# Mamba scan inside a transformer block: the output projection from f16 halves with a factor per chunk, one step later

## The chip, the core, the metric

The kernel runs on one core of a Trainium2 chip. Times are device microseconds of one execution. Before the change: median 766.98 us of 3 runs, 766.56 to 767.13.

## The reference, cut to what matters

```
x = x + 0.5 * ffn(layernorm(x))          # stage 1, dequantized 512x512 weight plus LoRA
h = layernorm(x)
h = h + mamba2(rmsnorm(h)) ; x = x + h + mlp(rmsnorm(h))     # stages 2 and 3
x = x + 0.5 * ffn(layernorm(x))          # stage 4
# in mamba2, 16 chunks of 128 tokens, 4 heads of 128:
Y = (att @ Xdt) + C @ state * exp(cs) + D * x ;  y = Y * silu(z) ;  return y @ w_out.T
```

x is 2048 tokens by 512, float32. `y @ w_out.T` is a product of 128 tokens by 512 with a 512x512 weight for each chunk: this is the output projection that the change is about.

## The kernel before, in words

Activations stay in SBUF with 128 partitions. Most products are computed from f16 halves: an f32 operand is scaled by a power of two and split into a high f16 part (ACT writes it) and a low part (DVE writes value minus high), and a product is hi*hi + hi*lo + lo*hi. The helper `product` (L1957) issues these three matmuls per block of 128 of the contraction; all of them are recorded at L1960. For four blocks that makes twelve matmuls of 512 columns.

The scan runs over 16 chunks, `step(c)`, c = 0 to 15, four chunks to a group i of 512 tokens, j = c mod 4. Every engine (`tensor`, `vector`, `scalar`, `gpsimd`, and `sync` for DMA) has its own list of instructions, written out by hand in a function `step(c)`; what an engine does is fixed in order, and semaphores (`e_...`) tie the lists. Work for later chunks is put between: stage 1 for chunk c+8 (`f`, `x1_stats`, `hi0`, `lo0`, `hi1`, `lo1`; steps 0 to 7 only), the input projections of group i+1 (`proj`, `SLOTS`: three, two, three and two of them in the steps j = 0 to 3; j = 0 has the dt columns, `steps`, as well), the convolution and gates of these (`conv`, `tanh` on ACT, `taps`, `silu`, `silu_z`, `softplus` on DVE), and in the last group the first gate/up products of stage 3 (`gate_up`). In steps 10 to 14 POOL also forms sums for Strassen's scheme in stage 3 (`sums`, `t_op`), DVE their low halves (`t_los`), and in steps 11 and 12 the halves of the first gate, up and down weights are cut (`cut_a`, `cut_b`).

One chunk goes this way. PE: `s1(c+1)`, `f`, `s2_diag` (L2056, needs the masked scores S from POOL), `s2_state` (L2065), `s2_inner` (L2073), `s1_bc(c+1)` (L2048), one projection or gate/up product, `w(c)` (L2083), the other projections. DVE: `gate_y` (L1425) multiplies Y by the gate, in place and in f32; `advance` (L1432) makes the next state; `weights` (L1406), `scan1` (L1415) make the next scores; POOL masks them and adds the diagonal (`scan_d`, L553, L555). `w(c)` is four f32 matmuls from y and the f32 `w_out`. `residual2(c)` (L1441) adds the normalized input n1 to it and `square` (L803), `rms2` (L559, L521), `hi2` (L794), `lo2(c)` (L1376) and a DMA transpose (`t2`, L457) make the next stage's input, hi2 and lo2 in step c+1.

PSUM banks 0 to 2 rotate among f, w and the projections in the order of `PLAN` (L289 to 320); a product waits until what used its bank three products before has been read.

Of the kernel before, what the change touches and what calls it, by code (L numbers as in the profile page):

```python
# [27 lines left out]
def build(nc, x_in, w_in_t, conv_w, conv_b, a_log, d_skip, dt_bias, w_out_t, ln1_w, ln2_w,  # L28
# [23 lines left out]
    with ctx:  # L52
# [8 lines left out]
        w_out = sb("w_out", [P, H, DM])  # L61
# [17 lines left out]
        homes = [gated_home(t) for t in (stage[:, 0:2048], stage[:, 2048:4096], w_out[:, :, :].rearrange("p h n -> p (h n)"))]  # L79
# [56 lines left out]
        q_raw = early.bitcast(I32)[:, 0:KB, DM:2 * DM]  # L136
        wf = early[:, KB:2 * KB, DM:2 * DM]
# [71 lines left out]
        wv = sb("wv", [P, 2, H])  # L209

# [11 lines left out]
        DT_AT, COL_AT, ROW_AT = 2 * P, 2 * P + 32, 3 * P  # L222

# [21 lines left out]
        def tokens_of(t, c):  # L245
# [15 lines left out]
        e_x_bn, e_x_var, e_x_rstd, e_x_scale, e_n0_hi, e_n0_lo, e_n0_tr = (  # L261
            sem(n) for n in "e_x_bn e_x_var e_x_rstd e_x_scale e_n0_hi e_n0_lo e_n0_tr".split())
        e_n0T, e_ffn, e_x1, e_x1_bn, e_x1_var, e_rms1, e_hn_scale = (
            sem(n) for n in "e_n0T e_ffn e_x1 e_x1_bn e_x1_var e_rms1 e_hn_scale".split())
# [10 lines left out]
        e_x2, e_ssq, e_ms, e_rms2, e_h2_hi, e_h2_lo = (  # L275
            sem(n) for n in "e_x2 e_ssq e_ms e_rms2 e_h2_hi e_h2_lo".split())
# [6 lines left out]
        e_scx, e_wscale, e_dsx, e_descale, e_c_var, e_c_rstd, e_c_scale = (  # L283
            sem(n) for n in "e_scx e_wscale e_dsx e_descale e_c_var e_c_rstd e_c_scale".split())
        e_cn_hi, e_cn_lo, e_cffn, e_c_bias, e_out, e_c_bn = (
            sem(n) for n in "e_cn_hi e_cn_lo e_cffn e_c_bias e_out e_c_bn".split())
# [19 lines left out]
        for c in range(NCH):  # L306
            i, j = divmod(c, CH)
            if c + 2 * CH < NCH:
                put(("f", c + 2 * CH), (e_x1, c + 2 * CH + 1))
            if c == 2 * CH + 2:  # L310
                put(("mx", 0), (e_scx, 1))
            if i + 1 < NS:
                put_proj(i + 1, SLOTS[j][0])
# [3 lines left out]
            put(("w", c), (e_x2, c + 1), None if i + 1 < NS else B_P[2])  # L317
            if i + 1 < NS:
                for q in SLOTS[j][1:]:
                    put_proj(i + 1, q)  # L320
# [77 lines left out]
        def _(sp_):  # L398
# [23 lines left out]
            sp_.dma_start(w_out[:, :, :], w_out_t.rearrange("(h p) n -> p h n", p=P)).then_inc(s_wout, 16)  # L422

# [3 lines left out]
            sp_.dma_start(ln2[:, :], ln2_w).then_inc(s_small, 16)  # L427
            gate_v = gate_t.rearrange("(k p) f -> p k f", p=P)
# [50 lines left out]
            for c in range(NCH):  # L479
# [6 lines left out]
                if c > 0:  # L486
                    t2(c - 1)
                if a < NCH:
                    t1(a)
                    next_x(a)  # L490
            t2(NCH - 1)
# [20 lines left out]
        def _(po):  # L512
# [13 lines left out]
            def ln0(c, j):  # L526
                po.wait_ge(e_x_var, c + 1)
                rsqrt(r0[:, c:c + 1], mv0[:, c, 2:3]).then_inc(e_x_rstd, 1)
                po.wait_ge(e_x_rstd, c + 1)
# [8 lines left out]
            def ln1_chain(c, j):  # L538
                po.wait_ge(e_x1_var, c + 1)
                rsqrt(r1[:, c, :], mv1[:, c, 2:4]).then_inc(e_rms1, 1)  # L540
                po.wait_ge(e_rms1, c + 1)
# [14 lines left out]

            def rms2(c, j):
                po.wait_ge(e_ssq, c + 1)
                po.tensor_scalar(ms[:, c:c + 1], ssq[:, c:c + 1], DOWN / DM, EPS * DOWN, ALU.mult, ALU.add).then_inc(e_ms, 1)  # L559
                po.wait_ge(e_ms, c + 1)  # L560
# [13 lines left out]
            chain(po.memset(ones3[:, :], 1.0))  # L574
            chain(po.memset(ident[:, :], 0.0))
# [48 lines left out]
            def step(c):  # L624
                a = c + 2 * CH
                if a < NCH:
                    ln1_chain(a, a % CH)
                if c + 1 < NCH:
                    scan_c(c + 1, (c + 1) % CH)
                    scan_d(c + 1, (c + 1) % CH)  # L630
                if a + 1 < NCH:
# [3 lines left out]
                early_sums = c in (3 * CH, 3 * CH + 1)  # L635
                if early_sums:
                    sums(c)
                rms2(c, c % CH)
                if not early_sums:
                    sums(c)  # L640

            def sums(c):
                for n in T_EARLY.get(c, ()):
# [4 lines left out]
                       3 * CH + 1: range(12, 16), 3 * CH + 2: range(16, 20)}  # L648
# [67 lines left out]
            for n in range(4, N_TOP):  # L716
# [13 lines left out]
            def c_norm(c, k):  # L730
                po.wait_ge(e_c_var, c + 1)
                rsqrt(rC[:, c:c + 1], mvC[:, c, 2:3]).then_inc(e_c_rstd, 1)
                po.wait_ge(e_c_rstd, c + 1)
# [23 lines left out]
        def _(ac):  # L757
# [43 lines left out]
            def square(c, j):  # L801
                ac.wait_ge(e_x2, c + 1)
                ac.activation(junk[:, :], x2[:, j % 2, :], ACT.Square, accum_out=ssq[:, c:c + 1]).then_inc(e_ssq, 1)  # L803

# [123 lines left out]
            def step(c):  # L928
# [11 lines left out]
                if a + 1 < NCH:  # L940
                    hi0(a + 1, (a + 1) % CH)
                if c > 0 and i_late < NS:
                    for q in late[1:]:
                        slot_b(i_late, q)
                if 0 < c <= 3 * CH:
                    hi2(c - 1, (c - 1) % CH)
                if c + 1 < NCH:
                    scan_decay(c + 1, (c + 1) % CH)
                if c > 3 * CH:
                    hi2(c - 1, (c - 1) % CH)  # L950
                if j == 2 and i + 1 < NS:
                    slot_a(i + 1, SLOTS[j][0])
                if a < NCH:
                    hi1(a, a % CH)
                if c + 1 < NCH:
# [3 lines left out]
                renorm(c)  # L959
                if c == 3 * CH + 2:  # L960
                    t_his(1, 0, 1, 2, 3)
                if i + 1 < NS:
                    if j != 2:
                        slot_a(i + 1, SLOTS[j][0])
                    slot_b(i + 1, SLOTS[j][0])
                    if j == 0:
                        sp_exp(i + 1)
                else:
                    gate_a(0, j)
                    gate_b(0, j)  # L970
                square(c, j)
# [9 lines left out]
            def prologue():  # L981
# [1432 lines left out]
```

## Time and profile before

| | |
|---|---|
| profiled execution | 768.65 us, its span 766.9 us |
| PE busy | 755.4 us, 98% of the span |
| DVE, ACT, POOL busy | 626.5, 446.4, 337.2 us |
| granted TensorE clock | full in all 40 slices |
| w_out's DMA, 1024 KB | 12.5 us from issue to landing |
| fourth block of the ffn weight made | at 18.5 us (DVE L1311, start 17.82, 0.69 long) |
| a DMA transpose of h2n_p | 2.7 us to landing in the median |

PE's matmuls are pipelined: the record of one reaches into the next, so what one costs in the stream is the difference between the starts. An f32 matmul is two records. The scan's steps take up the span from about 88 to 338 us, stage 3 follows, stage 4 is the end.

### The profile page before, as it was taken

The numbers are of one execution on the slowest core, as the hardware profiler recorded it, in microseconds if no ns is written. First come the engines' busy times: TensorE is split into PE (matmuls) and PEld (weight loads), VectorE is DVE, ScalarE is ACT, GpSimd is POOL, SyncE is SP. The second block draws the span as 40 slices with busy tenths as digits, with TensorE's granted clock in tenths as the row PEclk, the third lists the DMA queues.
The fourth block names the chain that finished last, engine by engine and source line by source line (L and its number), as shares of the span: only waits on it lengthen the run. The fifth ranks groups of instructions, "written<-read, shape, count | busy, mean of one in ns | idle before, by whom it ended". The sixth has DMA issues, their size and how long they took to land.

```text
span 766.9 us, 10654 instructions
## 1 busy us (share of the span) xinstructions
PE 755.4 (98%) x3469; PEld 353.2 (46%) x3470; DVE 626.5 (82%) x1230; ACT 446.4 (58%) x881; POOL 337.2 (44%) x392
## 2 busy tenths in 40 slices
PE   8999999999999999999999999999999999999998
PEld 3444554454555444444443444444444444444443
DVE  6888878878878979878799978878878878767994
ACT  3877767766686766643545556456456456444441
POOL 5631534663442379775413333233233233224574
PEclk9999999999999999999999999999999999999999
DMA  8843543552321211420521743743743743443565
GB/s 311 171 75 71 139 94 83 110 111 60 78 56 28 42 38 42 114 55 1 124 47 23 172 77 64 163 77 62 164 77 65 162 77 66 79 77 69 119 169 138
DMA packets 95414, 71.86 MB, mean 94 GB/s; under 512 B 65232, under 2 KB 72400, under 8 KB 95360
## 3 DMA queue, kind: packets, MB, share of 16 engines
q0 software_dynamic: 17280, 31.46, 23.0%
q1 hardware_dynamic: 77600, 39.66, 19.5%
q8 instruction: 28, 0.46, 0.2%
q14 instruction: 26, 0.21, 0.1%
q10 hardware_dynamic: 480, 0.07, 0.1%
HBM read 20.32 MB, written 4.19 MB: 32 GB/s over the span
## 4 chain that ended last, share of the span: by engine, by line
PE 77%; DVE 13%; ACT 4%; issue 3%; POOL 2%; DMA 1%; ACTq 0%; POOLq 0%; DVEq 0%
PE PS L1960 64%; PE PS L2083 4%; PE PS L2183 3%; DVE raw L1450 2%; PE PS L2091 1%; DVE stage L1450 1%; PE PS L2056 1%; DVE state L1432 1%; PE PS L2065 1%; DVE st L1289 1%; PE PS L2073 1%; PE PS L2048 1%; DVE xs L1382 1%; DVE S L1415 1%; DMA h<-lora_b_t 1%
## 5 line engine op out<-in xcount | busy, mean ns | idle before, releaser
L712 POOL DMA_DIRECT2D xs<-x x59 | 50.9, 864 | 151.2 <-ACT x L1159 137.1
L1960 PE MATMUL PS<-h,w_in 128*128 128x512 f16 x480 | 108.7, 379 | 0.2 <-issue 0.2
L1960 PE MATMUL PS<-h,x_t 128*128 128x512 f16 x408 | 94.0, 379 | 0.0
L1960 PEld LDWEIGHTS PS<-h,w_in 128*128 128x128 f16 x480 | 46.9, 98 | 65.3 <-issue 15.5
L1960 PE MATMUL PS<-n_T,stage 128*128 128x512 f16 x288 | 71.5, 379 | 0.0
L1159 ACT ACTIVATE x<-PS,d_d 128x512 f32<-128x512 f32 x59 | 40.2, 682 | 39.1 <-PE PS L1960 39.1
L1960 PEld LDWEIGHTS PS<-h,x_t 128*128 128x128 f16 x408 | 39.5, 98 | 48.5 <-issue 2.3
L521 POOL TENSOR_TENSOR r<-mv,mhalf 128x1 f32<-128x1 f32 (+1 forms) x32 | 29.4, 917 | 72.2 <-DVE mv L1293 55.0
L712 POOL DMA_DIRECT2D xs<-n x29 | 25.2, 868 | 71.1 <-ACT n L1159 60.8
L1960 PE MATMUL PS<-pre,stage 128*128 128x512 f16 x192 | 49.3, 379 | 0.0
L1129 ACT ACTIVATE xds<-tm,dgh 128x512 f32<-128x512 f32 x24 | 17.3, 722 | 53.0 <-DVE tm L1889 53.0
L1960 PEld LDWEIGHTS PS<-n_T,stage 128*128 128x128 f16 x288 | 28.1, 98 | 34.0 <-ACT x L1159 0.3
L1960 PE MATMUL PS<-w_ffn,raw_gu 128*128 128x512 f16 x192 | 43.2, 379 | 0.0
L1450 DVE SCALAR_TENSOR_TENSOR raw<-pre,cw,raw 128x512 f32<-128x512 f32 x36 | 28.0, 777 | 10.4 <-ACT raw L885 10.1
L1960 PE MATMUL PS<-raw,x_t 128*128 128x512 f16 x144 | 34.7, 379 | 0.4 <-DVE Ld L1842 0.4
L1960 PE MATMUL PS<-w_in,x_t 128*128 128x512 f16 x144 | 34.8, 379 | 0.0
L1159 ACT ACTIVATE n<-PS,d_d 128x512 f32<-128x512 f32 x29 | 19.8, 683 | 23.8 <-PE PS L1960 22.5
L1960 PE MATMUL PS<-h,n 128*128 128x512 f16 x144 | 33.2, 379 | 0.3 <-DVE n L1530 0.3
L2083 PE MATMUL PS<-w_out,stage 128*128 128x512 f32 x64 | 29.3, 600 | 0.3 <-DVE stage L1425 0.2
L1960 PEld LDWEIGHTS PS<-pre,stage 128*128 128x128 f16 x192 | 18.7, 98 | 22.7 <-ACT x L1159 0.3
L1960 PEld LDWEIGHTS PS<-w_ffn,raw_gu 128*128 128x128 f16 x192 | 18.7, 98 | 22.7 <-DMA raw_gu<-h2n_p 0.3
L2083 PE MATMUL PS<-w_out,raw 128*128 128x512 f32 x64 | 29.0, 595 | 0.1
(314 smaller groups left out, 1819.3 us busy)
## 6 DMA issues: line engine op xcount, KB each, us to landing
xs<-x POOLq DMA_DIRECT2D x75, 256.0 KB, 3.3
xs<-n POOLq DMA_DIRECT2D x29, 256.0 KB, 3.3
x_t<-x_in SPq DMA_DIRECT2D x16, 256.0 KB, 3.0
x_t<-hb POOLq DMA_DIRECT2D x16, 256.0 KB, 3.8
out<-x_t SPq DMA_DIRECT2D x16, 256.0 KB, 2.3
raw_gu<-gate_t SPq DMA_DIRECT2D x7, 512.0 KB, 4.4
raw_gu<-up_t SPq DMA_DIRECT2D x7, 512.0 KB, 6.6
raw_d<-down_t SPq DMA_DIRECT2D x7, 512.0 KB, 7.3
```

The source lines that it names most:

```text
L521: return po.tensor_tensor(dst, src, mhalf[:, 0:src.shape[-1]], ALU.pow)
L712: po.dma_start(chunk_of(xs, c), d_tmps[d % 3], accum_op=ALU.add).then_inc(s_acc[d % 3], 16)
L1129: ac.activation(th_s[ab], u4 if ab else c11, ACT.Tanh, scale=dgh[:, p % 2:p % 2 + 1]).then_inc(e_tanh_g, 1)
L1159: ac.activation(d_tmps[d % 3], bank(d_bank(d)), ACT.Copy, scale=d_d[:, p % 3:p % 3 + 1]).then_inc(e_ev, 1)
L1289: link(ve.bn_stats(stat, src), e_link, base + 1)
L1382: link(ve.scalar_tensor_tensor(chunk_of(xs, c), bank(b), 0.5 / ACT_SCALE if c < NF else d_f[:, :], x_t[:, j, :], ALU.mult, ALU.add), e_x1, ...
L1415: last = ve.scalar_tensor_tensor(S[:, s, h, :], heads(B_G)[:, h, :], dt[:, (c // CH) % 2, j * H + h:j * H + h + 1], Ld[:, h, :], ALU.mult, ...
L1432: last = ve.scalar_tensor_tensor(state[:, h, :], state[:, h, :], ecs[:, s, h, P - 1:P], heads(B_SS)[:, h, :], ALU.mult, ALU.add)
L1450: ins = ve.scalar_tensor_tensor(xbc[i % 2][:, b, :], pre[:, w, k:k + ST], cw[:, b, k:k + 1], xbc[i % 2][:, b, :], ALU.mult, ALU.add)
L1960: ins = pe.matmul(out_, lhs(a, b, k), rhs(a, b, k), start=first and n == 0, stop=last and n == len(todo) - 1)
L2083: last = pe.matmul(bank(b), y[:, h, (c % CH) * P:(c % CH + 1) * P], w_out[:, h, :], start=h == 0, stop=h == H - 1)
L2183: last = pe.matmul(bank(B_P[c % 2]), nT32[c % 2][:, k, :], wf[:, k, :], start=k == 0, stop=k == KB - 1)
```

## The change

- `w_out` is kept as two f16 halves. Its DMA goes to a raw place and is issued later, behind the making of the ffn weight. In the prologue ACT sums the absolute values of each row (`wo_sum`), DVE turns the sum into a power of two per partition (`wo_scale`), ACT writes the high half (`wo_hi`), DVE the low half (`wo_lo`, four times). `gate_y` multiplies by the inverse of that factor.
- y of a chunk is scaled by a factor of the chunk: ACT squares and sums y (`y_sum`), PE spreads the sum over all partitions with an f32 matmul of one column (`y_over`, into the bank of the state product), DVE reads it (`y_max`), POOL takes it to the powers -0.5 and 0.5 (`y_scale`), ACT writes y's high half (`y_hi`), DVE the low one (`y_lo`).
- `w(c)` is a `product` of these halves, twelve f16 matmuls, and stands in step c+1 behind `s1_bc`, ahead of the projections. `renorm(c)`, `residual2(c)` and `square(c)` go to step c+1 as well, residual2 ahead of `advance`; `rms2`, `hi2`, `lo2` and the transpose go to step c+2. `residual2` multiplies by the chunk's factor on the way.
- `s2_inner` waits for `y_max` of the chunk before, where it waited for `advance`.
- POOL's sums of step 14 move behind the scan; `sums` is always the last of a step. `w(15)` stands behind the fifth gate/up product.
- Some links of an engine with itself use the engine's own counter instead of a semaphore each.

```diff
-        w_out = sb("w_out", [P, H, DM])
+        w_out = sb("w_out", [P, 2, H, DM], F16)
...
+            def y_scale(c):
+                po.wait_ge(e_ym, c + 2)
+                po.tensor_tensor(y_s[:, c, :], y_m[:, c, :], halves[:, :], ALU.pow).then_inc(e_yscale, 1)
...
+                if c > 1:
+                    rms2(c - 2, c % CH)
                 if a < NCH:
                     ln1_chain(a, a % CH)
                 if c + 1 < NCH:
                     scan_c(c + 1, (c + 1) % CH)
                     scan_d(c + 1, (c + 1) % CH)
+                y_scale(c)
...
-                early_sums = c in (3 * CH, 3 * CH + 1)
-                if early_sums:
-                    sums(c)
-                rms2(c, c % CH)
-                if not early_sums:
-                    sums(c)
+                sums(c)
...
+            def y_sum(c):
+                ac.wait_ge(e_y, c + 1)
+                if c > 1:
+                    ac.wait_ge(e_ssq, c - 1)
+                ac.activation(junk[:, :].rearrange("p (h t) -> p h t", h=H), y_of(c), ACT.Square, accum_out=ssy[:, c:c + 1]).then_inc(e_ysum, 1)
+
+            def y_hi(c):
+                ac.wait_ge(e_yscale, c + 1)
+                if c > 0:
+                    ac.wait_ge(e_wo, c)
+                ac.activation(y_hl[:, 0, :, :], y_of(c), ACT.Copy, scale=y_s[:, c, 0:1]).then_inc(e_yhi, 1)
...
+            def y_max(c):
+                ve.wait_ge(e_yall, c + 1)
+                ve.tensor_scalar(y_m[:, c, :], PS[:, B_SS, 0:1].broadcast_to([P, 2]), Y_TINY, None, ALU.max).then_inc(e_ym, 1)
+
+            def y_lo(c):
+                cols = slice((c % CH) * P, (c % CH + 1) * P)
+                ve.wait_ge(e_yhi, c + 2)
+                ve.scalar_tensor_tensor(y_hl[:, 1, :, :], szs[(c // CH) % 2][:, :, cols], y_s[:, c, 0:1], y_hl[:, 0, :, :],
+                                        ALU.mult, ALU.subtract).then_inc(e_ylo, 1)
...
-                if 0 < c <= 3 * CH:
-                    lo2(c - 1)
+                if c > 0:
+                    residual2(c - 1, (c - 1) % CH)
+                if 1 < c <= 3 * CH:
+                    lo2(c - 2)
                 advance(c, j)
...
-                if j == 2 and i + 1 < NS:
-                    residual2(c, j)
+                y_max(c)
                 if i + 1 < NS:
                     slot_a(i + 1, SLOTS[j][0], {1: 9}.get(j))
...
                 else:
                     gate_up(0, j)
-                if j != 2 or i + 1 == NS:
-                    residual2(c, j)
+                y_lo(c)
...
                 pe.wait_ge(e_xds, c + 1)
                 if c > 0:
-                    pe.wait_ge(e_state, c)
+                    pe.wait_ge(e_ym, c + 1)
...
-                pe.wait_ge(e_y, c + 1)
+                pe.wait_ge(e_ylo, H + c + 1)
                 pe.wait_ge(*freed)
-                for h in range(H):
-                    last = pe.matmul(bank(b), y[:, h, (c % CH) * P:(c % CH + 1) * P], w_out[:, h, :], start=h == 0, stop=h == H - 1)
-                last.then_inc(e_wo, 1)
+                product(bank(b), lambda a, b, h: y_hl[:, a, h, :], lambda a, b, h: w_out[:, b, h, :], H).then_inc(e_wo, 1)
+
+            def y_over(c):
+                pe.wait_ge(e_ysum, c + 2)
+                pe.wait_ge(e_state, c + 1)
+                pe.matmul(PS[:, B_SS, 0:1], ssy[:, c:c + 1].broadcast_to([P, P]), over[:, :], start=True, stop=True).then_inc(e_yall, 1)
...
                 if c + 1 < NCH:
                     s1_bc(c + 1)
+                if c > 0:
+                    w(c - 1)
...
-                    for q in SLOTS[j][1:]:
+                    for n, q in enumerate(SLOTS[j][1:]):
                         proj(i + 1, q)
+                        if n == 0:
+                            y_over(c)
```

## Rows read from the trace of the kernel before

**Rows 1.** The page: busy time of each engine.
```profile
PE 755.4 (98%) x3469; PEld 353.2 (46%) x3470; DVE 626.5 (82%) x1230; ACT 446.4 (58%) x881; POOL 337.2 (44%) x392
```

**Rows 2.** Timeline of PE, steps 5 and 6: start, duration, line, operation.
```profile
175.01 2.75 PE L1960 MATMUL PS<-w_ffn,n_T 128*128 128x512 f16 x12
177.60 1.02 PE L2056 MATMUL PS<-S,tm 128*128 128x512 f32 x2
...
181.07 2.75 PE L1960 MATMUL PS<-h,w_in 128*128 128x512 f16 x12
183.92 3.70 PE L2083 MATMUL PS<-w_out,raw 128*128 128x512 f32 x8
187.46 2.75 PE L1960 MATMUL PS<-h,w_in 128*128 128x512 f16 x12
...
199.15 0.29 PE L2012 MATMUL PS<-dA,tri 128*128 128x16 f32 x2
199.29 0.43 PE L2013 MATMUL PS<-tri,dA 128*80 128x128 f32 x2
```

**Rows 3.** Timeline of PE: two waits, in steps 10 and 12.
```profile
253.71 0.27 PE L2124 MATMUL PS<-ident,mx 128*3 128x128 f32 x1 [0.52 <-ACT raw L885]
...
284.21 1.13 PE L2056 MATMUL PS<-S,tm 128*128 128x512 f32 x2 [1.02 <-POOL S L555]
```

**Rows 4.** Stretches: steps 1-7, 8-11, 12-15; length, busy time of each engine.
```profile
106.40:223.30 116.90, 116.52 (x542) 57.88 (x541) 98.74 (x239) 84.82 (x192) 56.14 (x69) 1.00 0.38 78
223.30:282.60 59.30, 58.43 (x289) 29.38 (x288) 49.06 (x114) 40.51 (x101) 24.55 (x28) 1.00 0.20 41
282.60:338.00 55.40, 54.35 (x225) 26.61 (x224) 46.62 (x77) 32.72 (x72) 46.06 (x44) 1.00 0.31 70
```

**Rows 5.** Timeline of DVE: taps, lo2, advance, weights, and cut_b's first part.
```profile
234.19 2.33 DVE L1450 SCALAR_TENSOR_TENSOR raw<-pre,cw,raw 128x512 f32<-128x512 f32 x3 [1.13 <-ACT raw L885]
236.43 0.23 DVE L1573 SCALAR_TENSOR_TENSOR sp<-PS,d_i,dtb 128x16 f32<-128x16 f32 x1
...
248.45 0.75 DVE L1376 SCALAR_TENSOR_TENSOR h2n_p<-x,r,h2n_p 128x512 f16<-128x512 f32 x1
249.11 1.12 DVE L1432 SCALAR_TENSOR_TENSOR state<-state,ecs,PS 128x128 f32<-128x128 f32 x4
250.15 0.16 DVE L1406 TENSOR_TENSOR wv<-Ld,dt 128x4 f32<-128x4 f32 x1
...
299.50 2.64 DVE L1509 SCALAR_TENSOR_TENSOR x_t<-raw_gu,sw,x_t 128x512 f16<-128x512 f32 x2
```

**Rows 6.** Timeline of POOL: a two-column pow, scan_d of step 9, sums of step 11.
```profile
200.92 1.09 POOL L521 TENSOR_TENSOR r<-mv,mhalf 128x2 f32<-128x2 f32 x1 [5.63 <-DVE mv L1293]
...
251.44 0.63 POOL L553 TENSOR_SCALAR_AFFINE_SELECT S<-S 128x512 f32<-128x512 f32 x1 [5.68 <-DVE S L1415]
252.16 1.27 POOL L555 TENSOR_TENSOR S<-S,d_diag 128x512 f32<-128x512 f32 x1
...
285.83 1.53 POOL L678 TENSOR_TENSOR h2n<-n_p,h2n 128x512 f32<-128x512 f32 x1
...
291.57 1.27 POOL L549 TENSOR_TENSOR raw<-raw,ecs 128x512 f32<-128x512 f32 x1
```

**Rows 7.** Timeline of ACT: a squared sum, a high half.
```profile
283.54 0.63 ACT L803 ACTIVATE junk<-x 128x512 bf16<-128x512 f32 x1 [2.01 <-DVE x L1441]
...
287.75 0.72 ACT L794 ACTIVATE h2n_p<-x,r 128x512 f16<-128x512 f32 x1
```

**Rows 8.** Line L1376 alone, ns min/median/max; then its group from 88 to 338.
```profile
L1376 DVE SCALAR_TENSOR_TENSOR h2n_p<-x,r,h2n_p x16: 735/752/2519, 115.6 to 336.5; 128x512 f16<-128x512 f32 x16
...
L1376 DVE SCALAR_TENSOR_TENSOR h2n_p<-x,r,h2n_p 128x512 f16<-128x512 f32 x16 | 17.3, 1081 | 5.0 <-ACT h2n_p L794 4.9
```

**Rows 9.** Timeline of ACT in the prologue: two waits for PE.
```profile
45.38 0.20 ACT L864 ACTIVATE pre<-hist 128x3 f32<-128x3 f32 x1 [3.11 <-PE PS L1960]
...
70.34 0.20 ACT L883 ACTIVATE pre<-hist 128x3 f32<-128x3 f32 x1 [3.57 <-PE PS L1960]
```

More of the change, by code:

```diff
@@ L209, in build @@
         wv = sb("wv", [P, 2, H])
+        y_hl = sb("y_hl", [P, 2, H, P], F16)
+        over = sb("over", [P, 1])
+        halves = sb("halves", [P, 2])
+        ssy = sb("ssy", [P, NCH])
+        y_m = sb("y_m", [P, NCH, 2])
+        y_s = sb("y_s", [P, NCH, 2])
+        wo_s = sb("wo_s", [P, 4])
         PS = ctx.enter_context(nc.psum_tensor("PS", [P, 8, 512], F32))
@@ L574, in _ @@
             chain(po.memset(ones3[:, :], 1.0))
+            chain(po.memset(over[:, :], 2.0 ** (-2 * Y_TOP)))
+            chain(po.memset(halves[:, 0:1], -0.5))
+            chain(po.memset(halves[:, 1:2], 0.5))
             chain(po.memset(ident[:, :], 0.0))
@@ L715, in _ @@
                 step(c)
-            for n in range(4, N_TOP):
+            rms2(NCH - 2, CH - 2)
+            for n in range(2):
+                t_op(2, n)
+            rms2(NCH - 1, CH - 1)
+            for n in range(2, N_TOP):
                 t_op(2, n)
@@ L949, in step @@
                 if c > 3 * CH:
-                    hi2(c - 1, (c - 1) % CH)
+                    hi2(c - 2, c % CH)
+                y_late = j != 2 and c < 2 * CH - 1
+                if not y_late:
+                    y_sum(c)
                 if j == 2 and i + 1 < NS:
@@ L954, in step @@
                     hi1(a, a % CH)
+                if y_late:
+                    y_sum(c)
+                if c > 0:
+                    square(c - 1, (c - 1) % CH)
                 if c + 1 < NCH:
@@ L969, in step @@
                     gate_a(0, j)
+                    y_hi(c)
                     gate_b(0, j)
-                square(c, j)
                 if i + 1 < NS:
@@ L1176, in _ @@
                 step(c)
+            hi2(NCH - 2, CH - 2)
+            gate_a(0, EARLY_GU)
+            renorm(NCH - 1)
+            gate_b(0, EARLY_GU)
+            square(NCH - 1, CH - 1)
             hi2(NCH - 1, CH - 1)
-            gate_a(0, EARLY_GU)
-            gate_b(0, EARLY_GU)
             for part in range(3):
@@ L1917, in c_out @@
                 ve.scalar_tensor_tensor(o_t[k], bank(k), d_f[:, :], chunk_of(xs, c), ALU.mult, ALU.add).then_inc(e_out, 1)
+            lo2(NCH - 2)
             gate_up(0, EARLY_GU)
+            residual2(NCH - 1, CH - 1)
             scale_read(1)
```

132 lines of the change are left out of this document (83 added, 49 removed).

## The prediction

> **What bounds the kernel now.** I read the page first: PE is busy 755.4 of 766.9 us [rows 1], so whatever TensorE issues less of is worth its time, as long as nobody makes it wait. Then TensorE's timeline through one step of the scan; the reader is to take the difference between one start and the next, not the durations, since matmuls overlap [rows 2]. Twelve f16 matmuls run from 175.01 to 177.60, 2.59 us. The scan's products of step 5 and the next chunk's score product run from there to 181.07, 3.47 us. The projection behind them takes 183.92 - 181.07 = 2.85, of which 2.59 is its twelve matmuls and 0.26 is waiting for the gated y. The output projection, four f32 matmuls in eight records, takes 187.46 - 183.92 = 3.54 us.
>
> Third, TensorE's own waits in the scan. They are short; two of the longest stand in steps 10 and 12, 0.52 and 1.02 us, the second ahead of L2056, where a step's masked scores come from DVE through POOL [rows 3]. So behind a full TensorE there is a second chain that is nearly as long. Fourth, the stretches [rows 4]: DVE is busy 98.74 of 116.90 us in steps 1 to 7, 49.06 of 59.30 in steps 8 to 11 and 46.62 of 55.40 in steps 12 to 15, 84, 83 and 84%. POOL is at 48% in the first and at 83% in the last. The bound is PE, with DVE two to three microseconds per step below it.
>
> **The change, part by part.**
> *The projection.* Twelve f16 matmuls for four f32: 3.54 - 2.59 = 0.95 us where these rows stand. The other bound is 0.88: the 3.47 us above are three f32 products of 512 columns and one of four times 128, so nearly the same work without the change of kind. I take 0.90 for sixteen, 14.4 us off PE.
> *The factor's matmul* (y_over, sixteen). One f32 matmul with one moving column. The nearest row is L2012 with 16 columns: 199.29 - 199.15 = 0.14 us [rows 2]. Bounds 0.1 and 0.29, the latter the whole duration of L2012's record. At 0.14, 2.2 us. PE's work thus falls by 12.2 us (between 9.4 and 13.6).
> *DVE.* Per chunk it gains y_lo, the same form as lo2 (249.11 - 248.45 = 0.66 in the stream), and y_max, a 128x2 read of PSUM: 0.2, by the 128x4 row's 0.16; bounds 0.1 and 0.4. residual2 becomes 0.07 longer. About 0.95 us a step. In steps 1 to 15 DVE then needs 194.4 + 14.3 = 208.7 us of what would be 231.6 - 11.4 = 220.2 on PE: 95% [rows 4, 5].
> *ACT* gains y_sum (0.63, and a read of the accumulator) and y_hi (0.72): 21 us over the scan, beside idle time of 32.1, 18.8 and 22.7 [rows 4, 7]. *POOL* gains a two-column pow, 1.09, in the stream 1.15 [rows 6].
> *Prologue.* The weight's absolute sum and its high half are 2048 columns on ACT each, some 2.5 us by four of the 512-column row; the low halves are four 0.66 on DVE. I count them at nothing: ACT stands idle 3.11 us ahead of 45.38 and 3.57 ahead of 70.34 [rows 9], exactly where the two are put, and the weight's DMA, issued when the fourth ffn block is made (18.5) and landing 12.5 later (table), is there before 42. Without that cover they cost up to 3 us; I keep 1 in the range.
> *Semaphores that become links within an engine* (statistics, rsqrt): the same waits, nothing, within 1 us either way.
>
> **What is queued where.** The factor ties the engines together inside a step. y_over(c) on PE stands behind the step's second projection, 7.8 us after the score product of c+1 (w and two projections), and waits for advance(c) and y_sum(c). DVE's y_max(c) waits for it, in front of the taps of the step's first projection; the next state product waits for y_max(c). Old DVE ran from gate_y(c) into advance(c) without needing more of PE; now residual2(c-1) stands before advance, and waits for w(c-1), 2.59 us behind the score product.
>
> I walked the four queues, each instruction starting at the later of "engine free" and "wait met", durations from rows 2, 5, 6 and 7.
> Steps 8 and 9: let the score product of step 8 end at 0. w ends at 2.6, a projection at 5.2, the dt columns (1.2) at 6.4, a projection at 9.0, y_over at 9.1. y_max 9.4; three taps, 2.24 to the next start, 11.6; three softplus links 0.6; y_lo 12.8; silu 13.4. Then DVE waits for ACT's conv of the next projection (y_hi and tanh ahead of it) until 13.9; two groups of taps with softplus, 2.4 each, and gate_y 0.66: 19.4. Two silus with 0.7 of waiting for tanh between them 21.2; residual2 21.9, lo2 22.5, advance (1.04) 23.6, scan1 (four like advance's) 24.7; POOL's mask and add, 2.0 us from 251.44 on [rows 6]: 26.7. PE reaches that product at 24.1 and stands 2.6 us, against 0.5 before. What was saved on PE in these two steps is gone.
> Step 12: y_max(11) stands behind cut_a, so y_scale(11) begins only then, and behind it on POOL the four sums, 285.83 to 291.57, 5.7 us [rows 6]. rms2(10) follows them, then hi2(10), and in step 12 the decay, lo2(10) and advance wait for that: 1.8 us at y_over(12). In step 13 advance stands behind cut_b, 2.64 us in its first part alone [rows 5]: another 1.8; then 0.9 for y_lo.
> All steps: 2.6 us given back in steps 0 to 7 (1.4 of it at y_over(6)), 2.0 more in 8 to 11, 8.8 in 12 to 15 and at the exit to the second stage, 13.4 in all. Sum: -12.2 + 13.4 = +1.2 us. The profiled execution took 768.65 (766.9 and 1.75 around it), which becomes 769.85; it lies 1.67 above the median of 766.98, so the median becomes 768.2.
>
> *A rule against the change.* lo2's form takes 0.735 us at the least, 0.752 in the median, 2.519 at the most, and sixteen of them were busy 17.3 us, mean 1.08 [rows 8]; the long ones lie beside POOL's tensor operations. By this mean y_lo, which has the same form, costs 16 x (1.08 - 0.75) = 5.3 us more than I counted. The Trainium skill ("SBUF — State Buffer", section "Who interferes with whom") says that a Vector instruction with two SBUF inputs and a GpSimd instruction that reads SBUF exclude one another for a whole instruction. The trace agrees in direction. What the walk leaves out is which new low halves meet a sum; that is rival B.
>
> **The rivals.**
> (A) *PE stays fed.* For it: PE's busy time lacks only 0.4, 0.9 and 1.1 us of the three stretches [rows 4], and the additions to ACT and POOL find idle time. Against: DVE needed at 95%. If some 5 of the 12.2 us are given back: -7 us, 760.
> (B) *The new low halves meet POOL's sums* (the other side). Place: steps 10 to 15, where POOL is 83% busy. Price: the 5.3 us, two thirds of them not hidden since each also delays advance or scan1: 3.5 on the forecast's 1.2, 771.7. It decides once DVE has no idle time left in a step, above 1 us of lengthening per step.
> (C) *The exit.* w(15) and the last rms2, hi2, lo2 come behind one more gate/up product; the last transposed chunk is needed two products (10.4 us) after w(15). Chain: residual2 0.7, square 0.7, rms2 0.9, hi2 0.7, lo2 0.7, the transpose 2.7 (table): 6.4. It holds unless POOL's sums, 1.3 each, stand in front. Late: +3 us, 771.
> (D) *It doesn't do what it says*: w stays at 3.5 us, twelve weight loads costing what the f32 passes did. The f16 products in rows 2 speak against it. +13.4 + 1.2, of which waits hide half: 775.
>
> **How the numbers follow.** What this measurement tells from no change is 0.2%, 1.5 us: 765.5 to 768.5. Forecast (saving given back, -2.5 to +4 about +1.2) 0.46: faster 0.07, same 0.24, slower 0.15. A 0.29: all faster. B 0.15, C 0.07, D 0.03: slower but for 0.02, which is same. Faster 0.36, same 0.26, slower 0.38. Range: down to 759, A with part of its tail; up to 774, B with the upper bounds of y_max and the prologue. The likeliest case alone is 764.5 to 771.
>
> **What would show it.** Right: w at L1960 and 2.59 us per chunk; PE's waits in the scan at about 13 us, most of them in steps 12 to 15, ahead of L2056, y_over and w; DVE over 90% busy in the scan; DVE waiting for PE at y_max in the steps with dt columns; steps 8 and 9 no shorter than before. Wrong: PE waiting under 8 us in the scan, so that DVE's idle time was slack and not queue, with a time of 762 or less; or waits that stand behind the last chunk.

## The result, and the profile after

| | before | after |
|---|---|---|
| median | 766.83 us (766.56 to 767.13, 4 runs) | 785.43 us (783.55 to 786.39, 4 runs) |
| profiled execution, its span | 768.65, 766.9 us | 786.39, 784.4 us |
| PE busy | 755.4 us, 98% | 753.0 us, 96% |

The ratio is 1.0236, 95% interval 1.0224 to 1.0248: slower by 18.6 us, where 768.2 was forecast and 774 was the upper end of the range.

The page after, busy time of each engine (it answers [rows 1]), and the granted clock in 40 slices:

```profile
PE 753.0 (96%) x3565; PEld 353.7 (45%) x3566; DVE 643.1 (82%) x1271; ACT 471.1 (60%) x932; POOL 358.9 (46%) x411
...
PEclk9999999999998999999999999999999999999999
```

PE's busy time fell by 2.4 us only, and the 13th slice, 235 to 255 us, has a lower clock. The three stretches of [rows 4], after, cut at the same instructions (length, busy us of PE, PEld, DVE, ACT, POOL; then granted clock, DMA share, GB/s):

```profile
102.05:218.11 116.06, 111.78 (x584) 57.19 (x582) 103.19 (x258) 95.42 (x219) 66.29 (x77) 1.00 0.39 78
218.11:283.74 65.63, 58.95 (x315) 30.32 (x314) 53.41 (x121) 44.20 (x109) 29.04 (x32) 0.95 0.18 37
283.74:351.14 67.40, 58.31 (x252) 27.75 (x251) 48.99 (x88) 39.60 (x88) 45.27 (x45) 0.92 0.32 63
```

They took 116.90, 59.30 and 55.40 us before. PE stands idle 4.3, 6.7 and 9.1 us in them, 20.1 in all, where it was 2.3. Fifteen w and fifteen y_over lie in them, so its busy time should have fallen by 11.4 us (15 times 0.76, w's 0.90 less y_over's 0.14) and fell by 0.3. What was saved was lost again, most of it at the lower clock.

Where the 17.5 us of span are, by marks that both timelines have. The dt columns of step 0 begin at 95.56 us (96.48 before): 0.9 earlier. Those of step 8 begin at 227.91 (230.13): 2.2 earlier. The first product of stage 3 begins at 359.33 (343.86): 15.5 later. The end is 17.5 later. So steps 8 to 15 with the exit lost 17.7 us and stage 3 another 2.0.

TensorE's timeline after, the new pieces and the waits (start, duration, line, operation; in brackets the idle time before, and its releaser):

```profile
99.36 0.28 PE L2169 MATMUL PS<-over,ssy 128*128 128x1 f32 x2
99.50 2.75 PE L2045 MATMUL PS<-h,w_in 128*128 128x512 f16 x12
...
108.67 2.75 PE L2045 MATMUL PS<-w_out,y_hl 128*128 128x512 f16 x12
111.26 1.03 PE L2045 MATMUL PS<-h,w_in 128*128 128x512 f16 x4
...
247.52 0.35 PE L2169 MATMUL PS<-over,ssy 128*128 128x1 f32 x2 [1.16 <-DVE state L1510]
...
249.67 0.38 PE L2211 MATMUL PS<-ident,mx 128*3 128x128 f32 x1 [1.32 <-DVE mx L1544]
250.60 2.08 PE L2141 MATMUL PS<-S,tm 128*128 128x512 f32 x2 [0.56 <-POOL S L565]
252.47 1.92 PE L2150 MATMUL PS<-stage,state 128*128 128x128 f32 x8
...
274.86 1.13 PE L2133 MATMUL PS<-raw 128*128 128x512 f32 x2 [3.08 <-DVE raw L1536]
...
286.38 1.67 PE L2141 MATMUL PS<-S,tm 128*128 128x512 f32 x2 [2.04 <-POOL S L565]
...
313.61 0.35 PE L2169 MATMUL PS<-over,ssy 128*128 128x1 f32 x2 [3.02 <-DVE state L1510]
313.82 4.44 PE L2045 MATMUL PS<-h,x_t 128*128 128x512 f16 x12
...
344.27 7.04 PE L2045 MATMUL PS<-h,x_t 128*128 128x512 f16 x24 [2.12 <-DVE pre L1879]
```

The reader is to see two things. The terms of the sum are there: y_over 0.14 us (99.36 to 99.50), w 2.59 us (108.67 to 111.26). And behind some of the waits the same products take up to twice as long: 2.08 us for 1.02 at 250.60, 4.27 for 2.59 between 313.82 and 318.09. The granted clock of such stretches (length, busy us of PE; then granted clock, DMA share, GB/s):

```profile
249.00:256.00 7.00, 5.77 (x14) 0.52 0.21 39
...
313.00:319.00 6.00, 5.39 (x22) 0.72 1.21 291
```

A mean of 0.52 means that the engine had the lower of its two levels, 1.2 of 2.4 GHz, for nearly all of this stretch.

### The profile page after: what moved, and what is told of

It reads as the page before. It is cut to its first block, busy times and chain, and to the rows that moved or that the text cites. A ratio compares the mean times of both kernels' runs of the same rounds, so it can differ in the third digit from the quotient of the medians.

```text
span 784.4 us, 11021 instructions
## 1 busy us (share of the span) xinstructions
PE 753.0 (96%) x3565; PEld 353.7 (45%) x3566; DVE 643.1 (82%) x1271; ACT 471.1 (60%) x932; POOL 358.9 (46%) x411
## 4 chain that ended last, share of the span: by engine, by line
PE 66%; DVE 18%; ACT 5%; issue 4%; POOL 4%; DMA 3%; SPq 0%; ACTq 0%; DVEq 0%; POOLq 0%
PE PS L2045 58%; DVE raw L1528 2%; PE PS L2176 1%; DMA raw_d<-down_t 1%; PE PS L2141 1%; PE PS L2150 1%; PE PS L2158 1%; PE PS L2133 1%; DVE state L1510 1%; DVE S L1471 1%; PE PS L2273 1%; DVE raw L1633 1%; POOL S L565 1%; DVE h2n_p L1432 1%; DVE stage L1528 1%
## 5 line engine op out<-in xcount | busy, mean ns | idle before, releaser
L2045 PE MATMUL PS<-h,x_t 128*128 128x512 f16 x408 | 98.0, 389 | 2.1 <-DVE pre L1879 2.1
L2045 PE MATMUL PS<-w_out,y_hl 128*128 128x512 f16 x192 | 44.1, 379 | 0.6 <-DVE y_hl L1482 0.6
L563 POOL TENSOR_SCALAR_AFFINE_SELECT S<-S 128x512 f32<-128x512 f32 x16 | 14.2, 890 | 45.0 <-DVE S L1471 45.0
L2045 PEld LDWEIGHTS PS<-w_out,y_hl 128*128 128x128 f16 x192 | 18.6, 98 | 28.8 <-issue 7.4
```

The costliest lines, as they stand in the source:

```text
L563: chain(po.affine_select(out=S[:, j % 2, :, :], in_=S[:, j % 2, :, :], compare_op=ALU.is_ge, fill=0.0, base=0, pattern=[[0, H], [1, P]], c ...
L2045: ins = pe.matmul(out_, lhs(a, b, k), rhs(a, b, k), start=first and n == 0, stop=last and n == len(todo) - 1)
```

## The experiments

All ratios are to the kernel before, in the same sessions; the brackets are 95% intervals. "Order" below means at which place of each engine's list the projection and what belongs to it stand. Differences between two changed kernels are differences of medians. The runs come from several sessions, in which the kernel before had medians of 766.77 to 767.32 us, so such a difference is good to about 0.5 us at best.

### Without the factor: e1_fixed

```diff
-                y_max(c)
-                y_scale(c)
-                    y_sum(c)
-                            y_over(c)
-                    pe.wait_ge(e_ym, c + 1)
+                    pe.wait_ge(e_state, c)        # s2_inner
```

> The changed kernel with the per-chunk factor left out: y_sum, y_over, y_max and y_scale are gone, y_s is a constant 1, and s2_inner waits for the advance again as before the change. The f16 halves, the step's delay of the projection and residual2 ahead of advance stay. Theory 1 (the factor's round trip PE - DVE - POOL - ACT inside a step, with what it holds up, makes most of the loss): 16 y_over at 0.14 are 2.2 us, and the waits at y_over (6.0 us in the scan) and most of those behind it go, so 770 to 774 us. Rival 2 (DVE simply has too much to do, and POOL's sums lengthen it): only 16 y_max of 0.07 to 0.15 go from DVE, the waits appear at L2141 and L2133 instead, 780 to 784 us.

779.86 us, 1.0152 [1.0121, 1.0183]. The factor costs 5.6 us of 18.6, its 2.2 us of y_over among them. That is outside the first theory and just below the range of the second: taken out alone, the round trip is not the greater part.

### The order alone: e2_f32late

```diff
-                product(bank(b), lambda a, b, h: y_hl[:, a, h, :], lambda a, b, h: w_out[:, b, h, :], H).then_inc(e_wo, 1)
+                for h in range(H):
+                    last = pe.matmul(bank(b), y[:, h, (c % CH) * P:(c % CH + 1) * P], w_out[:, h, :], start=h == 0, stop=h == H - 1)
```

and without y_hi, y_lo, wo_sum, wo_hi, wo_scale, wo_lo and the factor.

> The placement alone: the output projection is f32 again, straight from the gated y, without halves, factor or the prologue's work on the weight, but one step later, with residual2, square, rms2, hi2 and lo2 in the order of the changed kernel. Against the kernel before, the work of every engine is the same. If the placement costs nothing, 766 to 768 us. If residual2 ahead of advance, behind a product that starts after the score product, is what makes DVE late: 771 to 775 us.

785.28 us, 1.0226 [1.0199, 1.0253], far above both theories: with the work of the kernel before, the order costs as much as the whole change. This is the main finding. The waits of DVE in that kernel from 88 to 360 us (us in total, times, longest), then its timeline in step 12:

```profile
DVE x L1509 <- PE PS L2151: 17.7, 6, 5.3
```

```profile
292.23 0.69 DVE L1509 TENSOR_TENSOR x<-n,PS 128x512 f32<-128x512 f32 x1 [4.46 <-PE PS L2151]
292.83 0.76 DVE L1422 SCALAR_TENSOR_TENSOR h2n_p<-x,r,h2n_p 128x512 f16<-128x512 f32 x1
293.52 1.11 DVE L1500 SCALAR_TENSOR_TENSOR state<-state,ecs,PS 128x128 f32<-128x128 f32 x4
...
294.62 1.12 DVE L1461 SCALAR_TENSOR_TENSOR S<-PS,dt,Ld 128x128 f32<-128x128 f32 x4
```

And TensorE's timeline of the same kernel:

```profile
287.68 1.02 PE L2116 MATMUL PS<-raw 128*128 128x512 f32 x2
288.54 3.60 PE L2151 MATMUL PS<-w_out,stage 128*128 128x512 f32 x8
...
297.86 1.12 PE L2124 MATMUL PS<-S,tm 128*128 128x512 f32 x2
...
300.58 1.02 PE L2116 MATMUL PS<-raw 128*128 128x512 f32 x2
...
314.66 2.07 PE L2124 MATMUL PS<-S,tm 128*128 128x512 f32 x2 [4.00 <-POOL S L565]
```

From one score product (287.68) through w (288.54), residual2 (292.23), lo2, advance (293.52), scan1 (294.62), POOL's mask and the masked scores' product (297.86) to the next score product (300.58) it is 12.90 us, and a step there is 12.53 us of PE's work (286.93 to 299.46 in the kernel before). The output projection, which nothing of the scan waited for before, is now a link of the scan's own loop. DVE stands 4.46 us for it in this step and has its long pieces (the low halves of the sums, 296.56 to 302, and cut_b) behind that; two steps later PE waits 4.00 us for S. In the kernel before DVE waited 0.3 us for the projection from 88 to 340 us, and its longer waits were for ACT, ahead of the taps. Its line there, and the same place of step 12 in the kernel before:

```profile
DVE x L1441 <- PE PS L2083: 0.3, 1, 0.3
```

```profile
286.93 1.02 PE L2048 MATMUL PS<-raw 128*128 128x512 f32 x2
...
290.30 1.13 DVE L1415 SCALAR_TENSOR_TENSOR S<-PS,dt,Ld 128x128 f32<-128x128 f32 x4
```

Before, scan1 began 3.37 us behind the start of the score product; here it begins 6.94 us behind it. By itself the loop costs only 0.4 us in this step; what it takes is the time to spare, so that the next long piece on DVE reaches TensorE as a wait.

Where the time goes is read against v1_f32order below, which has the same work in the old order. The score product of step 8 begins 1.7 us later than there (222.19 and 220.46), that of step 12 7.0 later (287.68 and 280.72), of step 13 7.3, of step 14 12.4, and the first product of stage 3 17.1 (359.57 and 342.51). TensorE's waits of 2.23 us in step 11, 4.00 in step 14 and 2.12 at the exit, with the lower clock around them (0.58 in the mean from 312 to 320 us), make up a good part of this. Which moved piece causes which wait was not traced one by one.

### residual2 behind scan1: e3_resid

```diff
-                if c > 0:
-                    residual2(c - 1, (c - 1) % CH)
                 if 1 < c <= 3 * CH:
                     lo2(c - 2)
                 advance(c, j)
...
                     scan1(c + 1, (c + 1) % CH)
+                if c > 0:
+                    residual2(c - 1, (c - 1) % CH)
```

> The changed kernel with residual2(c-1) moved behind scan1(c+1) on DVE. advance and scan1 come 0.66 us earlier and no longer wait for the output projection (DVE waited 6.7 us for it in two steps of the scan). If this order is what makes y_over and the masked scores late (6.0 and 3.5 us of PE's waits in the scan): 778 to 782 us. If DVE's amount of work or the factor's chain makes them late: 784 to 787 us, since the work stays.

791.47 us, 1.0309 [1.0284, 1.0334]: worse by 6, outside both expectations. TensorE now waits for residual2 itself, since w's bank is one of three that rotate and the product three places on wants it. Its line from 60 to 430 us (waits in total, times, longest); the changed kernel has no such wait:

```profile
PE PS L2045 <- DVE x L1519: 5.0, 4, 1.8
```

### The clock: e5_warm

```diff
+            WARM = {9: 5, 13: 12}
             def y_over(c):
+                if c in WARM:
+                    pe.wait_ge(e_y, c + 1)
+                    warm(bank(B_YT), WARM[c])
```

> The changed kernel with idle f16 products of 512 columns put where PE waits longest and the granted clock then falls: 5 ahead of y_over(9), 5 ahead of bound_turn(0), 2 ahead of s2_diag(10), 8 ahead of s2_diag(12), 12 ahead of s1_bc(12), 12 ahead of y_over(13), 8 ahead of the fifth gate/up product. Their result is not used. They hold PE no longer than its waits there, within 1 us in all. If the stretches at half clock (some 8.6 us of lengthening between 240 and 350 us) follow from those waits: granted clock 1.00 there and 776 to 779 us. If the clock falls for another reason: no change, 785 to 787 us.

782.74 us, 1.0200 [1.0170, 1.0231]. The clock did what the first theory said, the time did not: 2.7 us, not 7 to 9. The first stretch and a later one (length, PE busy; then granted clock, DMA share, GB/s):

```profile
240.00:256.00 16.00, 15.45 (x74) 1.00 0.17 35
...
320.00:352.00 32.00, 30.02 (x140) 1.00 0.25 50
```

So the lower clock follows from the waits. The 52 idle products are 11.2 us of PE's 755.3 (at 2.59 us for twelve); the other 744.1 are 8.9 less than the 753.0 of the changed kernel, and 2.7 of these came through. The rest was waited again or held by the idle products themselves, which these runs don't tell apart. That DVE's chain is the bound there fits, but is not shown by this run.

### The old order, one chunk late: v1_f32order, and two orders between: e6_wfirst, x_res

```diff
@@ step(c) on TensorE, v1_f32order against e2_f32late
-                if c > 0:
-                    w(c - 1)
                 if i + 1 < NS:
                     proj(i + 1, SLOTS[j][0])
...
                     bound_spread(0)
+                if c > 0:
+                    w(c - 1)
@@ on DVE
-                if c > 0:
-                    residual2(c - 1, (c - 1) % CH)      # ahead of advance
...
+                if c > 0 and (j != 2 or i + 1 == NS):
+                    residual2(c - 1, (c - 1) % CH)      # behind the taps
```

> As e2_f32late (f32 projection of the chunk before, no factor, no halves), but every piece stands where it stood before the change: w(c-1) behind the step's first projection or gate/up product on TensorE, residual2(c-1) behind its taps on DVE, renorm, square and rms2 at their old places. Only the index is one less. Theory (where the work is put, w behind the score product and residual2 ahead of advance, which makes DVE wait 17.7 us for w, is the loss; lateness by itself costs nothing): 766 to 769 us. Rival (the projection of the chunk before is late wherever it stands, above all at the exit with w(15) behind the fifth gate/up product): 775 us or more.

768.35 us, 1.0013 [0.9997, 1.0028], the clock at 0.999. The cut above shows w and residual2; renorm and square on ACT and rms2 on POOL go back to their old places as well. The delay by a chunk, the new exit and the links together cost 1.0 us (-0.2 to 2.1); the places cost 16.9 by the medians. DVE still waits 5.5 us for w there, in four waits, but behind the taps and not ahead of advance. e6_wfirst changes only w against e2_f32late, to a third place ahead of the masked scores' product; x_res leaves w where the change has it and moves all the rest back:

> As e2_f32late, with one piece moved: w(c-1) stands ahead of the masked scores' product (s2_diag) of its step instead of behind the next score product, so that it is over before DVE comes to residual2. If DVE's wait for w (17.7 us in e2_f32late) is what makes the scan's chain late: that wait goes to under 3 us and the time to 770 to 775 us, the exit's 2.1 us ahead of the fifth gate/up product staying. If the other moves (residual2 ahead of advance, rms2 first on POOL, square ahead of scan2) carry the loss: 782 us or more.

> The fourth corner beside e2_f32late, e6_wfirst and v1_f32order (all f32, no factor): w(c-1) stands behind the next score product as in the changed kernel, residual2, square, renorm and rms2 at their places of before the change. If DVE's wait for w ahead of advance is the loss: the wait is gone, 768 to 772 us, little above v1_f32order. If w's place by itself costs (the step's first projection reaches ACT and DVE 3.4 us later): 775 to 780 us.

776.18 us, 1.0101 [1.0080, 1.0123], and 799.37 us, 1.0417 [1.0393, 1.0441]. In e6_wfirst DVE's wait for w is 1.4 us, as foreseen, but the time is above the range expected for that: DVE now waits 15.0 us at gate_y for the state's product, which stands 3.43 us later behind w, and PE waits 2.1 us at the fifth gate/up product. In x_res PE waits for the bank (its waits from 60 to 430 us: line, releaser, us in total, times, longest):

```profile
PE PS L2029 <- DVE x L1508: 15.7, 7, 3.6
```

My expectation for x_res missed the bank; both of its cases lie far below the result. w's place and residual2's belong together: an early w takes a bank early, residual2 must free it early, so it stands ahead of advance, and so the loop waits for w. With residual2 and the rest moved back alone 14 us are added to e2_f32late; with w at the third place 9.0 are left against the kernel before; with everything back 1.0. The fourth corner, w at its old place with residual2 ahead of advance, was not run, and residual2 was not parted from renorm, square and rms2.

### The halves: v4_halves, x_nolo, v7_same, v13_lomove

v4_halves is v1_f32order with the f16 product, y_hi and y_lo, and a constant factor. x_nolo is the changed kernel without y_lo.

```diff
@@ x_nolo, y_lo(c)
-                ve.scalar_tensor_tensor(y_hl[:, 1, :, :], szs[(c // CH) % 2][:, :, cols], y_s[:, c, 0:1], y_hl[:, 0, :, :],
-                                        ALU.mult, ALU.subtract).then_inc(e_ylo, 1)
+                ve.sem_inc(e_ylo, 1)
```

> v1_f32order with the f16 halves added and no factor (a constant 1 in its place): the projection of the chunk before from twelve f16 products, w, residual2, square, renorm and rms2 at the places of before the change, y_hi and y_lo after the chunk's gate, y_sum, y_over, y_max and y_scale left out. Against v1_f32order: w 16 times 0.84 less on TensorE (13.4 us), y_lo 0.66 a step more on DVE and y_hi 0.6 a step more on ACT. If the halves' own work fits into idle time once the order is right: 756 to 762 us, and the factor is what v2_order (780.6) pays for. If the extra DVE work by itself is too much for the scan: 766 to 775 us.

> The changed kernel with y_lo left out (its low half is zero from the start; w has its twelve products as before). DVE has 16 x 0.66 = 10.6 us less to do, the order and the factor's chain are those of the changed kernel. If the amount of work on DVE makes the loss: 772 to 778 us. If the places of w and residual2 make it: 783 to 786 us, DVE still waiting for w ahead of residual2.

766.85 us, 0.9989 [0.9976, 1.0003], and 781.44 us, 1.0186 [1.0169, 1.0203]. Against v1_f32order the halves save 1.5 us, where w is some 13.4 us shorter (16 times 3.43 less 2.59); the two intervals just meet, so even the 1.5 is hardly clear of noise. In the changed order they save 5.4 (e2_f32late to e1_fixed). Taking y_lo away from the changed kernel (DVE's busy time falls by 11.6 us) gives 4.0 back, which lies between the two theories. Two kernels tried w from halves with less delay:

```diff
@@ v7_same (the kernel before; w(c) in its own step)
                     scan1(c + 1, (c + 1) % CH)
+                y_lo(c)
@@ v13_lomove (v12_early; w(c-1) in step c)
                     scan1(c + 1, (c + 1) % CH)
+                if c > 0:
+                    y_lo(c - 1)
```

> The kernel before, with the output projection from f16 halves in the same step, by a constant 1 instead of the factor: y_hi(c) on ACT behind the decay, y_lo(c) on DVE behind scan1(c+1), w(c) at its old place; the weight's halves in the prologue as in the changed kernel. It shows whether the step's delay was needed. If y_lo comes in time behind the score product: the saving of w less a few waits, 758 to 764 us. If w now waits for y_lo in each step (gate, ACT, DVE and scan1 ahead of it): 768 to 776 us.

> v12_early with y_lo(c-1) behind scan1(c+1), ahead of the place where DVE waits for ACT's convolution, instead of behind the taps and residual2 of step c-1. The work is the same. If the place matters: up to 4 us less than v12_early. If the low half there meets POOL's mask and add and gets longer, or delays lo1 and the statistics: the same or up to 4 us more.

800.14 us, 1.0422 [1.0372, 1.0471], and 795.41 us, 1.0367 [1.0346, 1.0389]. Both far outside what was expected, for one reason, TensorE's wait for the low half ahead of w, in v7_same and then in v13_lomove:

```profile
PE PS L2006 <- DVE y_hl L1445: 35.7, 11, 5.3
```

```profile
PE PS L2045 <- DVE y_hl L1479: 32.8, 11, 5.4
```

At these places the low half comes too late; where it stands a step ahead of w (v4_halves), TensorE has no such wait. I had counted on DVE being at scan1 when PE ends the score product. In step 3 of v7_same the score product ends at 153.15 and DVE's scan1 begins at 155.07, 1.9 us behind, with the low half behind that until 156.8.

### The low half on POOL: v8_pool, v9_pool10

```diff
+            def y_lo(c):                                   # on POOL, behind ln0
+                po.wait_ge(e_yhi, c + 2)
+                po.tensor_tensor(y_hl[:, 1, :, :], szs[(c // CH) % 2][:, :, (c % CH) * P:(c % CH + 1) * P], y_hl[:, 0, :, :], ALU.subtract).then_inc(e_ylo, 1)
```

> v4_halves with y_lo moved from DVE to POOL (a 128x512 subtraction, 1.15 to 1.6 us by POOL's rows, behind ln0 of the step). DVE is rid of 16 x 0.66 = 10.6 us. If DVE's work in the scan is what eats the halves' saving: 757 to 762 us. If the masked scores (7.0 us of PE's waits in v4_halves stand ahead of them, through POOL) get later by POOL's new work, or contention lengthens DVE: 766 to 772 us.

> v8_pool with the low halves of chunks 10 to 15 back on DVE, since POOL has the sums there. If POOL's sums behind the low half are a cost: 1 to 4 us less than v8_pool. If DVE is short in those steps too: the same or more.

776.71 us, 1.0142 [1.0121, 1.0163], and 772.77 us, 1.0075 [1.0060, 1.0090]. v8_pool lies above both of its cases. DVE lost 12.4 us of y_lo (6.4 and 6.0), yet its busy time went from 641.7 to 637.7 only. Its taps and gate_y in v4_halves, then in v8_pool (busy us, mean ns, idle time before):

```profile
L1521 DVE SCALAR_TENSOR_TENSOR raw<-pre,cw,raw 128x512 f32<-128x512 f32 x36 | 27.5, 763 | 5.2 <-ACT raw L924 4.7
...
L1496 DVE SCALAR_TENSOR_TENSOR raw<-PS,wo_s,raw 128x512 f32<-128x512 f32 x8 | 6.0, 745 | 2.5 <-PE PS L2144 2.5
```

```profile
L1526 DVE SCALAR_TENSOR_TENSOR raw<-pre,cw,raw 128x512 f32<-128x512 f32 x36 | 31.9, 886 | 6.9 <-ACT raw L929 6.5
...
L1501 DVE SCALAR_TENSOR_TENSOR raw<-PS,wo_s,raw 128x512 f32<-128x512 f32 x8 | 6.0, 744 | 5.4 <-PE PS L2148 5.4
```

The taps, with two operands in SBUF, went from 763 to 886 ns in the mean; gate_y, with one operand in PSUM, stayed at 745. The Trainium skill ("SBUF — State Buffer", section "Who interferes with whom") says that a Vector instruction with two SBUF inputs contends with a GpSimd instruction that reads SBUF, and one with a single SBUF input, outside the two-port modes, does not. The two traces agree with it, by 886 against 763 ns and 744 against 745. v9_pool10, with the last six low halves back on DVE, gives 3.9 us back, within its range.

### The factor in the old order: v2_order, v3_later, v11_nowait

v2_order is the changed kernel in the old order; v3_later moves y_max behind the taps, y_scale behind ln0, y_hi behind tanh and y_lo to the next step; v11_nowait makes the factor and does not use it:

```diff
@@ v11_nowait, y_hi(c)
-                ac.wait_ge(e_yscale, c + 1)
+                ac.wait_ge(e_y, c + 1)
```

> The changed kernel with w(c-1), residual2(c-1), renorm, square and rms2 at the places where they stood before the change; f16 halves and factor as they are, y_sum, y_over, y_max and y_lo not moved. Theory (the loss is the order): the saving of w (14.4 us) less y_over (2.2) comes through in part, with DVE at its limit: 760 to 770 us. Rival (the factor's round trip and the low half cost what was forecast, whatever the order): 768 to 775 us.

> v2_order with the factor's chain taken out of the engines' way: y_max(c) behind the taps or the gate/up pair of its step, y_scale behind ln0 on POOL, y_hi behind tanh on ACT, y_lo(c) at the beginning of the next step on DVE. The work is that of v2_order. If waits in the factor's chain (ACT stood 27.7 us ahead of y_hi, DVE 4.7 us ahead of y_max) hold up what stands behind them: 3 to 6 us less than v2_order, 757 to 764 us. If only the amount of work on DVE counts: the same as v2_order within 1 us.

> v2_order with the factor made (y_sum, y_over, y_max, y_scale, with all their waits) but not used: y_hi, y_lo and residual2 take a constant 1, so that y_hi does not wait for POOL's power. If ACT's waits ahead of y_hi (26.4 us in v2_order) make the factor's 13.8 us: 767 to 770 us. If y_over and y_max (TensorE waits for y_sum and advance, DVE for y_over, 9.5 us) make them: 777 to 781 us.

780.63 us, 1.0159 [1.0136, 1.0182]; 783.46 us, 1.0193 [1.0167, 1.0219]; 777.53 us, 1.0144 [1.0129, 1.0160]. v2_order lies above both of its theories. Against v4_halves the factor costs 13.8 us in this order. ACT's wait for POOL's power, 26.4 us in v2_order, is worth 3.1 of it (v11_nowait); 10.7 stay, with TensorE waiting 5.7 us at y_over for advance and y_sum, and DVE 10.2 us at y_max. v3_later, which I expected to gain, lost 2.8: PE's waits ahead of the masked scores rose from 5.0 to 8.0 us. The factor's work and its tie are not told apart further.

Six of the kernels make a table of order and content, medians in us:

| | f32, no factor | halves, no factor | halves and factor |
|---|---|---|---|
| old order | 768.35 (v1_f32order) | 766.85 (v4_halves) | 780.63 (v2_order) |
| order of the change | 785.28 (e2_f32late) | 779.86 (e1_fixed) | 785.43 (the change) |

With the factor in place, the old order gives back only 4.8 us; in the order of the change, taking out the factor gives 5.6. Undoing both gives 18.6. Against v4_halves the order alone costs 13.0 us and the factor alone 13.8; each by itself spends what w saves, and neither alone explains the result.

### POOL's sums first: v12_early

```diff
+                early_sums = c in (3 * CH, 3 * CH + 1)
+                if early_sums:
+                    sums(c)
```

> v4_halves with one piece of the change undone on POOL: in steps 12 and 13 the four sums stand ahead of rms2 again, as before the change, and use the 4 us in which POOL waits for the square. If the mask of chunk 14 came late because the sums stood behind rms2 (3.65 us of TensorE's wait): 761 to 764 us. If another engine takes the place of that wait: 765 to 767 us.

766.76 us, 0.9990 [0.9978, 1.0002]: nothing, and the wait of 3.7 us at step 14 stayed. DVE's timeline there:

```profile
292.87 2.30 DVE L1584 SCALAR_TENSOR_TENSOR x_t<-raw_gu,sw,x_t 128x512 f16<-128x512 f32 x2
...
296.29 2.03 DVE L1883 TENSOR_TENSOR stage<-pre,stage 128x512 f16<-128x512 f32 x1
```

In v4_halves the same two took 1.41 and 0.68 us. The sums, moved earlier on POOL, now stand beside the first of them (291.13 to 293.95), and POOL waits 3.44 us for DVE's scores instead of the other way round.

No version beat the kernel before by more than a measurement can tell; v4_halves and v12_early are equal to it within 0.3%.

## Why the prediction was wrong

- *w at 2.59 us, y_over at 0.14, y_lo at 0.66 in the stream, y_max, the prologue at nothing.* Right, with w's saving a little smaller: the sixteen f32 projections of the kernel before took 3.475 us in the mean, so the saving is 0.885 each, not 0.90. y_max's record is 0.14 us, 0.07 in the stream (203.55 to 203.62), below its lower bound of 0.1. The prologue is 0.9 us shorter. DVE's busy time in the steps, 205.6 us, is near the 208.7 that were worked out; its share is 83%, not 95%, because the steps became longer.
- *What is given back.* This is the step that failed: the walk of the four queues, and in it the order. The term in the sum is 13.4 us; measured by the spans it is 29.7 (12.2 and 17.5; by the medians 30.8). Cut at the marks of [rows 4], with 0.76 us a step as the forecast saving, steps 1 to 7 gave back 4.5 us, steps 8 to 11 9.4 and steps 12 to 15 15.0; the forecast had 2.6, 2.0 and 8.8 (the first with step 0, the last with the exit). In kind it is 17.8 us more of idle PE in the three stretches (20.1 against 2.3), 11.1 us of busy time above the count there, and 2.0 in stage 3, less the 0.9 won in the prologue: 30.0, which leaves 0.3. Of the 11.1, up to 8.7 are the lower clock (5% of 65.63 and 8% of 67.40 us); by the starts of the slow products it is 7.8.
- *What the walk had wrong.* I saw that residual2 "waits for w(c-1), 2.59 us behind the score product", and that it stands before advance, but put no wait there, and did not close the loop from one score product to the next and compare it with a step of PE. In the changed kernel DVE waits there 7.3 us in three waits, the longest 3.9. The order by itself costs 18.4 us (e2_f32late) without any factor or low half, of which 16.9 are due to the places (v1_f32order). The loop shows why nothing was left to spare (12.90 us against 12.53 in the f32 kernel), not the size. The factor's tie was priced too low as well: in the old order it costs 13.8 us (v2_order against v4_halves).
- *Where the walk was near.* y_over(6): 1.4 us forecast, 1.17 measured. Steps 8 and 9: advance done 24.6 us behind the score product of step 8 by the trace, 23.6 by the walk; PE's waits there 1.16, 1.32 and 0.56, 3.0 us, where 2.6 was forecast. In steps 12 and 13 it missed: it had 1.8 us at y_over(12) and 1.8 in step 13, and the trace has 0.29 and 3.02. All idle time of PE in steps 12 to 15 is 9.1 us, near the 8.8, but 2.12 of it stand at a product that the walk did not name, and the lower clock comes on top.
- *What it left out.* Two waits for cs_b (2.7 us), 3.08 us at s1_bc(12) for a silu late on DVE (the three taps ahead of it took 3.08 us, 2.30 in the kernel before, and y_lo 1.64 for 0.75, beside POOL's sums; that these lengthened them is argued), 2.12 us at the fifth gate/up product, which w(15) used to cover, 2.04 us at a bound's transpose in stage 3 (0.55 before), and the clock. From the dt columns of step 0 to those of step 8 the time fell by 1.3 us where 6.1 was due, so 4.8 us were given back in steps 0 to 7, not 2.6.
- *The clock.* The sum had it at nothing, without a reason. It follows from the waits; filling them is worth 2.7 us (e5_warm).
- *Rival A* (PE stays fed): no. *Rival B* (the low halves meet the sums): not as priced: y_lo came to 13.2 us in sixteen, 1.2 above its median duration, where 5.3 was priced; three taps (3.08 us) and a silu (1.75) of step 11 were longer as well. *Rival C* (the exit): 2.0 us in stage 3 and 2.1 at the gate/up product, another wait than the one described. *Rival D* (w no shorter): no, w takes 2.59 us.
- *What I said would show it:* PE's waits of 13 us, mostly in steps 12 to 15: 20, and 11 of them ahead of step 12. The list named waits ahead of w, but not DVE's wait for w, ahead of residual2.

## What to carry to other kernels

When work is moved between the steps of a pipelined loop, write down the loop of the tightest recurrence with the moved piece in it, and compare it with the time of a step, before any saving is counted: here a piece that was off the loop became a link of it, and its move cost 16.9 us with unchanged work, more than the 12.2 us that the change saves on TensorE. A saving on the engine that is busy 98% of the time counts only as far as the other engines keep up: v4_halves turned 13.4 us into 1.5. A product and the instruction that frees its bank are moved together: moved apart, they cost 6 and 14 us here (e3_resid, x_res).

## What the runs showed that I had not expected

- Around waits of 1.16, 1.32 and 0.56 us TensorE's granted clock was 0.52 in a stretch of 7 us, and f32 products took 2.08 instead of 1.02 us; with idle products in the waits it stayed at 1.00, and still only 2.7 us were gained.
- Moving 12.4 us of work from DVE to POOL took 4.0 us off DVE.
- The factor costs 5.6 us in the changed order and 13.8 in the old one; the order costs 16.9 with the f32 product, 13.0 with the halves (e1_fixed against v4_halves) and 4.8 with halves and factor (the change against v2_order): the parts of this change cannot be added up.
